# Node batches of the third score pass split between that pass and two convolutions; one bias of the second score pass by TensorE

## What is computed

```python
x = _layernorm(x + _L0_gnn_ref(...))   # three attention layers
x = _layernorm(x + _L1_gnn_ref(...))   # relu(agg @ W1.T + b1), relu(agg @ W2.T + b2), agg with edge weights
x = _layernorm(x + _L2_gnn_ref(...))   # relu(agg(x @ W) + b), agg by degree
x = _layernorm(x + _L3_gnn_ref(...))   # two of relu(concat(h, mean of neighbours) @ W + b)
```

## Time and profile before

| | |
|---|---|
| three runs | 5124.89, 5128.42, 5132.35 us; median 5128.42 |
| profiled execution | 5132.61 us, its span 5130.8 us |
| busy in the span | PE 3927.6 (77%), DVE 3884.4 (76%), ACT 3424.7 (67%), POOL 2796.4 (55%) |
| mean granted clock of TensorE | 0.903 |
| first gather of edge rows: second and third score pass | 2041 and 2776 us |
| first gather: first, second, fourth, fifth convolution | 3580, 3839, 4365, 4624 us |

### The profile page before, as it was taken

One profiled execution on the slowest core, in us unless ns is written; L12 is line 12 of the kernel. 1 busy time (PEld: TensorE's weight loads), 2 busy tenths in 40 slices (PEclk: granted clock), 3 DMA queues, 4 the chain that ended last, 5 costly groups with the idle time before them and its releaser, 6 DMA issues. The chain is left out here.

```text
span 5130.8 us, 108022 instructions
## 1 busy us (share of the span) xinstructions
PE 3927.6 (77%) x23872; PEld 2892.8 (56%) x23872; DVE 3884.4 (76%) x14954; ACT 3424.7 (67%) x11259; POOL 2796.4 (55%) x2718
## 2 busy tenths in 40 slices
PE   2999999566996898774998995897767676665554
PEld 1666766344774454663555774343666666565554
DVE  4999999676998787997886998898547777444343
ACT  0899999454886676884776885787548788333332
POOL 2888888475552122651223452112767676777777
PEclk9999999787998899997999997998888888997666
DMA  2566665597996576994676995675546565543332
GB/s 62 165 187 196 202 194 190 194 331 274 355 353 220 196 242 209 328 326 152 228 241 234 349 350 189 221 225 170 157 152 202 187 208 189 156 146 113 96 97 72
DMA packets 612938, 1072.25 MB, mean 209 GB/s; under 512 B 107736, under 2 KB 128362, under 8 KB 612764
## 3 DMA queue, kind: packets, MB, share of 16 engines
q1 hardware_dynamic: 537308, 944.74, 54.2%
q0 software_dynamic: 75456, 125.65, 9.2%
HBM read 607.70 MB, written 466.24 MB: 209 GB/s over the span
## 5 line engine op out<-in xcount | busy, mean ns | idle before, releaser
L2409 POOL DMA_INDIRECT got_c<-table,src_row x980 | 931.3, 950 | 378.8 <-issue 296.5
L1410 POOL DMA_INDIRECT src_got_s<-table,src_row x588 | 554.4, 943 | 497.4 <-PE bank L1456 119.4
L1994 POOL TENSOR_TENSOR part_m<-part_m,half_sum_m 128x512 f32<-128x512 f32 x147 | 220.7, 1501 | 916.8 <-DVE half_sum_m L2210 916.8
L2437 PE MATMUL bank<-pick_c,got_c 128*128 128x128 f32 x1960 | 348.3, 333 | 407.9 <-DMA got_c<-table,src_row 337.2
L2003 PE MATMUL bank<-w_all,dt_m 128*128 128x512 f32 x1176 | 568.7, 600 | 35.4 <-DMA dt_m<-delta_t 33.6
L2437 PEld LDWEIGHTS bank<-pick_c,got_c 128*128 128x128 f32 x1960 | 299.9, 234 | 453.6 <-issue 251.6
L1565 ACT ACTIVATE z_s<-z_s,shift_s,dev_s 128x128 f32<-128x128 f32 x1176 | 483.4, 485 | 2.1 <-DVE shift_s L1684 0.9
L2540 ACT COPY agg_c<-bank 128x512 f32<-128x512 f32 x245 | 143.0, 584 | 434.7 <-DVE bank L1851 281.4
L790 PEld LDWEIGHTS bank<-w_mean,ht 128*128 128x128 f32 x2352 | 313.5, 194 | 144.0 <-issue 144.0
L2461 PE MATMUL bank<-w_c,agg_c 128*128 128x128 f32 x1960 | 389.3, 328 | 2.3 <-ACT agg_c L2540 2.2
L787 PE MATMUL bank<-bias,first_row 128*128 128x512 f32 x588 | 323.6, 632 | 38.1 <-ACT ht L850 13.8
(11 more groups left out here) (327 smaller groups left out, 11582.0 us busy)
## 6 DMA issues: line engine op xcount, KB each, us to landing
table<-rows SPq DMA_DIRECT2D x294, 256.0 KB
x_s<-table SPq DMA_DIRECT2D x294, 256.0 KB
x_c<-table SPq DMA_DIRECT2D x245, 256.0 KB
table<-mid_s SPq DMA_DIRECT2D x196, 256.0 KB
table<-z_s SPq DMA_DIRECT2D x196, 256.0 KB
table<-z_c SPq DMA_DIRECT2D x196, 256.0 KB
own_rows_s<-table SPq DMA_DIRECT2D x147, 256.0 KB
pick_t_s<-picks_t SPq DMA_DIRECT2D x147, 256.0 KB
```

The source lines that it names most:

```text
L1410: nc.gpsimd.indirect_dma_start(out=src_got[r][:, g, :], out_offset=None, in_=tables[l].rows, in_offset=bass.IndirectOffsetOnAxis(ap=src_ro ...
L2409: nc.gpsimd.indirect_dma_start(out=got[r][:, g, :], out_offset=None, in_=t_in.rows, in_offset=bass.IndirectOffsetOnAxis(ap=src_row[:, t:t ...
L2437: ins = nc.tensor.matmul(b_sum[r][:, k * P:(k + 1) * P], got[b.slot][:, k, :], pick[r][:, k, :], start=k == 0, stop=sage, skip_group_check ...
```

## The change

Three parts.

**Third score pass** (`solo=True`): only the even node batches (h = 0) are worked on, one for each edge batch, with step functions of its own for SP, PE, ACT and DVE and other waits for POOL. Buffers that belonged to h = 0 and 1 now alternate from batch to batch (`side`).

**First and fourth convolution** (`nodes`): the odd node batches. In every second turn (`even(b)`: b is even) one batch is loaded; offset 1 makes them 1, 3, ..., 49 in the first convolution, offset 49 makes them 49, 51, ..., 97 in the fourth, 25 each, 49 twice. They use banks 6 (for turning, hidden and turning back) and 7 (product). The new functions are node_turn, node_hidden, node_middle and node_product on PE, node_turned, node_relu, node_middle_out (copy of mid, copy of the bias), node_deviation and node_normalise on ACT, node_residual, node_moments and node_scale on DVE, load_nodes, store_node_middle and store_nodes on SP.

**Second score pass**: `set_by_dve` is (0,) where there is no first weight, so the bias of h = 1 is set by a matmul of 512 columns on PE in `product`, and `set_bias(b, 1)` is gone from DVE.

The diff, cut (step_solo stands four times, for SP, PE, ACT and DVE; node_steps twice, for PE and ACT):

```diff
-        def edge_scores(l, first, second, t_in, t_mid, t_out):
+        def edge_scores(l, first, second, t_in, t_mid, t_out, solo=False):
...
-                set_by_dve = (0, 1)
+                set_by_dve = (0, 1) if first else (0,)
...
+                def nth(b, h):
+                    return b if solo else b.twin(h)
+
+                def side(b, h):
+                    return b.half if solo else h
...
+                        def step_solo(at):
+                            b = at(0)
+                            if b:
+                                loads(b)
+                            b = at(5)
+                            if b:
+                                store_middle(b, 0)
+                                store_delta(b)
+                                store_score(b)
+                            b = at(6)
+                            if b:
+                                store_rows(b, 0)
...
                             if g == 0:
                                 pool.wait_ge(delta_made, b - 3)
+                            elif solo:
+                                if g == 1:
+                                    pool.wait_ge(h_made, b - 2)
+                                elif g == 2:
+                                    pool.wait_ge(y_made, b - 3)
+                                else:
+                                    pool.wait_ge(turned, b - 1)
...
                             if h in set_by_dve:
                                 pe.wait_ge(bias_set[h], b.count(1, 1))
                             else:
                                 hold(pe, z_read, n.count(1, -1))
-                                nc.tensor.matmul(b_y[h][:, :], first_row[:, :], b2[:, :], start=True, stop=False, skip_group_check=True)
+                                nc.tensor.matmul(b_y[side(b, h)][:, :], first_row[:, :], b2[:, :], start=True, stop=False, skip_group_check=True)
...
+                        def step_solo(at):
+                            b = at(1)
+                            if b:
+                                hidden(b, 0)
+                            b = at(2)
+                            if b:
+                                turn_delta(b)
+                                product(b, 0)
+                                turn_hidden(b, 0)
+                            b = at(3)
+                            if b:
+                                score(b)
+                            b = at(0)
+                            if b:
+                                turn_rows(b, 0)
+                            b = at(1)
+                            if b:
+                                spread(b)
...
+                        def step_solo(at):
+                            b = at(1)
+                            if b:
+                                relu(b, 0)
+                            b = at(3)
+                            if b:
+                                deviation(b, 0)
+                            b = at(2)
+                            if b:
+                                delta_out(b)
+                            b = at(3)
+                            if b:
+                                normalise(b, 0)
+                            b = at(0)
+                            if b:
+                                turn_out(b, 0)
+                            b = at(3)
+                            if b:
+                                score_out(b)
...
+                        def step_solo(at):
+                            b = at(3)
+                            if b:
+                                scale(b, 0)
+                            b = at(2)
+                            if b:
+                                residual(b, 0)
+                                middle(b, 0)
+                                moments(b, 0)
+                            b = at(1)
+                            if b:
+                                set_bias(b, 0)
+                                difference(b)
...
+                        def node_hidden(b):
+                            pe.wait_ge(nxt_made, b.ring(1))
+                            nc.tensor.matmul(b_turn[:, :], nw1[:, :], nxt[:, :], start=True, stop=True).then_inc(nh_made, 1)
...
+                        def node_steps(at):
+                            b = at(4)
+                            if even(b):
+                                node_middle(b)
+                            b = at(5)
+                            if even(b):
+                                node_product(b)
+                            b = at(3)
+                            if even(b):
+                                node_hidden(b)
+
                         def step_gcn_relu(at):
                             b = at(1)
                             if b:
                                 sum_edges(b)
+                            node_steps(at)
                             b = at(2)
                             if b:
                                 product(b)
+                            if even(b):
+                                node_turn(b)
                             b = at(1)
                             if b:
                                 add_own(b)
...
                                 add_own(b)
                                 sum_edges(b)
+                            node_steps(at)
                             b = at(2)
                             if b:
                                 product(b)
+                            if even(b):
+                                node_turn(b)
...
+                        def node_relu(b): 
+                            act.wait_ge(nh_made, b.ring(1))
+                            hold(act, ny_made, b.ring(1, -1))
+                            nc.scalar.activation(flat(nht), b_turn[:, :], ACT.Relu, bias=nb1[:, 0:1]).then_inc(nht_made, 1)
...
+                        def node_steps(at):
+                            b = at(3)
+                            if even(b):
+                                node_relu(b)
+                            b = at(4)
+                            if even(b):
+                                node_middle_out(b)
+                            b = at(6)
+                            if even(b):
+                                node_deviation(b)
+                            b = at(7)
+                            if even(b):
+                                node_normalise(b)
+
                         def step_relu(at):
                             b = at(0)
                             if b and not sage:
                                 diagonals(b)
+                            node_steps(at)
                             b = at(2 if sage else 1)
                             if b:
                                 set_bias(b)
                                 sums_out(b)
+                            b = at(2)
+                            if even(b):
+                                node_turned(b)
...
                             b = at(1)
                             if b:
                                 carry_over(b)
+                            b = at(6)
+                            if even(b):
+                                node_scale(b)
                             b = at(2)
                             if b:
                                 residual(b)
+                            b = at(5)
+                            if even(b):
+                                node_residual(b)
+                                node_moments(b)
```

More of the change, by code:

```diff
@@ L1565, in normalise @@
                                 ins = nc.scalar.activation(v[:, g, :], v[:, g, :], ACT.Identity,
-                                                           bias=shift[h][:, g:g + 1], scale=dev[h][:, g:g + 1])
+                                                           bias=shift[side(b, h)][:, g:g + 1], scale=dev[side(b, h)][:, g:g + 1])
                             ins.then_inc(z_made, 1)
@@ L2426, in _ @@
                         pe.wait_ge(w_in, 16 * n_w)
+                        if nodes:
+                            pe.wait_ge(nw_in, 64)
+                            nc.tensor.matmul(b_node[:, :], first_row[:, :], nb2[:, :], start=True, stop=True,
+                                             skip_group_check=True).then_inc(banks_open, 1)
                         for h in range(2):
@@ new lines, in node_middle_out, with node_deviation @@
+                        def node_middle_out(b):
+                            r = b.slot // 2
+                            act.wait_ge(nmid_turned, b.ring(1))
+                            hold(act, nmid_stored[r], b.ring4(16, -16))
+                            nc.scalar.copy(flat(nmid[r]), b_turn[:, :]).then_inc(nmid_made, 1)
+                            hold(act, nz_read, b.ring(1, -1))
+                            nc.scalar.copy(b_node[:, :], nb2[:, :]).then_inc(n_bias, 1)
+                        def node_deviation(b):
+                            r = b.slot // 2
+                            act.wait_ge(nz_stat, b.ring(1))
```

(13 more changed lines are left out.)

208 lines of the change are left out of this document (149 added, 59 removed).

## The result

| | before | changed |
|---|---|---|
| runs, one after the other on one chip | 5130.39 us median of 4 (5124.89 to 5142.55) | 5280.86 us median of 4 (5275.92 to 5282.05) |
| ratio to before, 95% interval | | 1.0289 [1.0262, 1.0316] |
| span of the profiled execution | 5130.8 us | 5280.1 us |
| mean granted clock of TensorE | 0.903 | 0.891 |

What follows compares the result with a forecast made beforehand. Each stage has its own limit: DVE and transfers in the second score pass, PE and transfers in the third, POOL's gathers in the first and fourth convolutions. -88 - 9 + 12 + 213 = +128 on 5132.6 gives 5260 us, range 5195 to 5325.

Steps and rivals of the forecast that it cites:

- Direction and place: Kernel slower, chiefly in the fourth convolution, where PE and ACT would take turns: +213 us there, +128 in all.
- the clock in the fourth convolution: Fourth convolution: PE's clock taken as 0.84, making 18.2 us for two turns and +201 us before the stage's end.
- rival 2: Fourth convolution at the fifth's clock, 0.68: +277 in place of +213, kernel 5325 us; chance 0.15.
- the end of the node chain: First and fourth convolutions: the last node batch's steps after the last edge batch stay unhidden, 12 us each.
- the loop as written: Third score pass: a loop through DVE takes 5.5 us a turn; 5.65 taken, -88 us after 4 for lag.
- the floor: Second score pass: unchanged transfers keep the turn at 6.2 us or more, so only -9 us (0 to -30).
- the floor of 5.6 for the third pass: Third score pass: seven transfers of 0.66 us each need 5.6 us a turn.
- First convolution: Stage stays POOL's, 0 in the loop; only the last node batch's end adds, +12 us (+8 to +40).
- Rival 1: Fourth convolution keeps the full clock: +169 there, +84 in all, kernel 5217 us; chance 0.20.
- my own sign for the size: Fourth convolution: a granted clock of 0.78 to 0.86 would confirm the forecast's size.
- Rival 4: Third score pass does not gain, PE and DVE waiting on each other, turn 7 us; kernel 5328 us; chance 0.05.
- Rival 3: Fourth convolution stays POOL's, node work costing only its tail: -73 in all, kernel 5060 us; chance 0.05.

Runs made afterwards that it cites:

- the kernel with the sums first: The changed kernel, but in the fourth convolution ACT's copies of bias, own rows and sums precede the node work: 5048.10 us in the second group, 5667.89 in the first group.
- the kernel with normalise alone moved: The changed kernel, but in the fourth convolution only node_normalise goes behind ACT's copies of the sums: 5796.26 us in the first group, 5805.1 in the third.
- The kernel with the bias alone: The kernel before, with only the second score pass's second bias set by PE: 5113.44 us, ratio 0.9972, in the second group; ratio 1.0006 in the first group.
- the second group: Follow-up kernels run one after the other on one chip; the kernel before took 5130.83 us there, the changed kernel 5285.83 us.
- the first group: Follow-up kernels run one after the other on one chip with uneven transfers; the kernel before took 5643.35 us there, the changed kernel was not run.
- the third: Group of follow-up kernels on one chip with uneven transfers; the kernel before took 5640.99 us there, the changed kernel 5857.65 us.

## Why the prediction was right, and where not

**Direction and place: right.** The fourth convolution was forecast to turn serial for the reason given: agg_c behind nht_c in ACT's one list, PE working to node_hidden and stopping. The trace shows the two waits at 3.78 and 2.87 us (4.0 and 3.1 forecast; ACT's terms as written add up to 4.01 and 3.12, not 3.97 and 3.1, which changes nothing) and the gathers waiting for PE. That the order is the cause is shown, not argued, by the kernel with the sums first.

**The mis-sized term: the clock in the fourth convolution.** Forecast 18.2 us for two turns from PE's 9.33 us at a clock of 0.84 and ACT's 7.07; measured 20.45, of which 6.65 us are PE's two waits and 13.8 its work. With the granted clock of 0.75 the same sum gives 9.33 / 0.75 + 7.07 = 19.5. The other 0.9 us come from the form of the term: the granted clock is a mean over time and the low stretches lie on the products, not on the waits. 13.8 us of work for 9.33 is a rate of 0.68, the number that I had used only for rival 2. The stage came out nearer to that rival (+277) than to the forecast (+213): it took +253, of which 242 lie before the last edge batch's residual and 11 behind it, the end of the node chain (12 forecast). The full loop would give half of 20.45 less 5.0, times 49, or +256; the first two pairs of turns, with the pipeline not yet full, took 15.1 and 14.5 us and give back 11 of it. The waits read from the rows were right and the choice of 0.84, close to the first convolution, was not: with two waits in a pair of turns PE is back at the full rate only for 0.6 us at node_middle and for the 3.7 us from node_turn to node_hidden (4450.68 to 4454.4). The Trainium skill ("TensorE: Matmul & The Clock Gate", its section on HAM oscillation) has a kernel whose every wait for data put the following matmuls back to half rate. The changed kernel's trace agrees with it, at its waits of 3.78 and 2.87 us; in the kernel with normalise alone moved not every wait does so, as the products at full rate behind its 2.88 us show.

The total is only 21 us off where this stage is 40 off. That is luck in part: the two score passes gained 15 us more than forecast, the first convolution lost 3 more, and 7 came from stages in which the change does nothing.

**Third score pass: right, 6 us better.** The turn is 5.3 to 5.4 us (150 gathers in the 200 us from 2800), where 5.5 was the loop and 5.65 my choice; so the loop as written was already 0.1 to 0.2 too long. The waits of the changed kernel from 2800 to 3000 us show its meetings, PE waiting for DVE and DVE for PE:

```profile
PEld bank L1503 <- DVE delta_s L1714: 43.3, 27, 1.9
ACT ht_s L1596 <- PE bank L1459: 39.6, 36, 1.3
DVE z_s L1727 <- PE bank L1482: 38.1, 37, 1.4
```

**Second score pass: the size was wrong, -9 against -18.5.** The step that failed is the floor: "the transfers are unchanged and need 6.27 us". The same eight transfers now take 6.0 us a turn, at a share of 1.00. So the share times the turn, 6.27 us before, was no floor and is no price per transfer; what the 0.27 us were isn't shown. The kernel with the bias alone has the whole of the gain (20 us), two thirds of the 30 that the copy's own time would give. It follows that the floor of 5.6 for the third pass, worked out from the same 0.66 us, was wrong too: the turn came out below it.

**First convolution: right.** +15.5 for +12. The turn is 4.9 us, no more than before, so there is nothing in the loop. The last gather starts 245 us after the stage's mark in both kernels; the last residual comes 4 us later than before, and from it to the next stage 11 us more pass, the end of the node chain. The last edge batch's residual is at 3722.69 us, and the last normalise ends at 3734.5:

```profile
3722.69 0.69 DVE L2836 TENSOR_SCALAR z_c<-bank 128x512 f32<-128x512 f32 x1
```

```profile
3732.82 1.65 ACT L2751 ACTIVATE nz_c<-nz_c,nshift_c,ndev_c 128x128 f32<-128x128 f32 x4 [0.44 <-DVE nshift_c L2891]
```

**The rivals.** Rival 1, the full clock, falls with the 0.75, and so does my own sign for the size, a clock of 0.78 to 0.86. Rival 4 falls with the third pass's turn of 5.4 us. Rival 3, the fourth convolution staying POOL's at 5060 us, is what the sums-first kernel does in the second group: 5048. What was held against it, the copies behind relu in one list, is just what that edit removes. The stages in which the change does nothing are 7 us shorter in sum; I know no cause for that, and with the spread of the runs it needs none.

## What to carry to other kernels

Work that fills idle time must not stand in an in-order list ahead of what another engine waits for: ahead of the copies it cost 235 us more here than behind them, with the same instructions (512 against 277 us, where the stage without it takes 259). Read for each moved step at which lag the engines hand over; the first convolution, where the sums are copied one step before product takes them, bore the same list with a turn no longer than before. And when such waits cut PE's work into short bursts, price what follows each wait at half rate, not all of the work at the mean clock of a milder stage: here 6.0 us behind one wait and 3.2 behind the other ran at half rate, and half of that is the 4.5 us between 9.33 and 13.8.

## What the runs showed of the hardware

- **Filling a stage can raise the clock.** The first convolution ran at 0.86 before and at 1.00 with the node work in its gaps (3550 to 3650 us), at the same turn of 4.9 us.
- **The rate behind a wait is not a matter of that wait alone** (2.88 us, full rate; 2.95 us, half rate, in one kernel 16 us apart). What else decides was not tried.
- **The same program took 10% longer in two of the three groups**, with transfers that come in fits. The record names chip 9 for the first group and the second, and chip 8 for the third, so this number alone doesn't tell the two kinds apart. Here is the kernel with the bias alone in its fourth convolution, 200 us in 40 slices each (tenths of the DMA engines' time, and GB/s), in the first group:

```profile
DMA  3516453265542361634535516426173454416434
GB/s 122 179 30 207 105 180 121 82 188 163 157 143 53 115 185 28 210 105 131 168 91 177 168 52 195 107 83 204 40 225 90 140 194 123 134 39 202 112 134 158
```

```profile
DVE z_c L2613 <- DMA out_dram<-z_s: 65.2, 10, 6.8
```

and in the second group:

```profile
DMA  5554555555555555455554555545554555455432
GB/s 158 153 155 157 153 157 157 157 157 157 156 159 157 154 156 158 156 154 157 153 163 147 158 151 156 167 139 164 159 175 138 150 161 165 145 153 164 142 103 84
```

Again and again a slice of 5 us moves a fifth or so of what its neighbours do, and DVE waited ten times for some 6.5 us until a store had landed. What holds them up isn't shown by the trace. A stage bound by its own chain doesn't notice (the change's fourth convolution, 525 us against 512), one bound by gathers does (306 against 259). The changed kernel is slower than sums-first by 235 us of stage in one kind of group and by 193 in the other, but the sums-first kernel's gain of 1.7% over the kernel before is a loss of 0.5% in the first group. Against the kernel with the bias alone there, sums-first gains 40 us in the third score pass (429.6 against 469.2), where it is 94 in the second group, and pays 28 and 26 us in the two convolutions, where it is 17 and 17.
